# Two transformer blocks: products of the second part and the conditioning of layer 0 issued among the turns of the tiles

## What is computed

```
ada = silu(c) @ W_ada + b_ada
shift_msa, scale_msa, gate_msa, shift_mlp, scale_mlp, gate_mlp = split(ada, 6)
h = layernorm(x) * (1 + scale_msa) + shift_msa
q, k, v = heads(h @ W_qkv + b_qkv)
x = x + gate_msa * (softmax(q * D**-0.5 @ k.T) @ v @ W_proj + b_proj)
```

## Time and profile before

| | us |
|---|---|
| median of three runs | 892.95 |
| lowest, highest | 891.84, 893.7 |
| the profiled execution: its time | 893.41 |
| its span | 891.4 |
| PE busy | 781.1 (88%) |
| DVE busy | 643.1 (72%) |
| ACT busy | 525.9 (59%) |
| POOL busy | 281.8 (32%) |

### The profile page before, as it was taken

One profiled execution on the slowest core, in us unless ns is written; L12 is line 12 of the kernel. 1 busy time (PEld: TensorE's weight loads), 2 busy tenths in 40 slices (PEclk: granted clock), 3 DMA queues, 4 the chain that ended last, 5 costly groups with the idle time before them and its releaser, 6 DMA issues.

```text
span 891.4 us, 16501 instructions
## 1 busy us (share of the span) xinstructions
PE 781.1 (88%) x6096; PEld 363.8 (41%) x6096; DVE 643.1 (72%) x1277; ACT 525.9 (59%) x731; POOL 281.8 (32%) x369
## 2 busy tenths in 40 slices
PE   1569889999988989899898999999979986999996
PEld 0235222222221222222234465566646654566555
DVE  4849888898887898888936955746688897764531
ACT  4433577777776677777785725635547734634640
POOL 4311011325554241102023337241223565342122
PEclk9979799999999999999999999999989996999998
DMA  7302011110111110000040011101676730000000
GB/s 221 83 22 74 21 29 28 28 48 12 41 43 50 45 28 21 21 22 21 2 110 2 11 41 42 22 18 49 155 178 161 175 66 28 8 28 1 26 26 27
DMA packets 52127, 45.35 MB, mean 51 GB/s; under 512 B 23898, under 2 KB 41236, under 8 KB 52055
## 3 DMA queue, kind: packets, MB, share of 16 engines
q1 hardware_dynamic: 47613, 36.35, 15.9%
q10 hardware_dynamic: 4442, 8.04, 2.8%
HBM read 27.66 MB, written 9.46 MB: 42 GB/s over the span
## 4 chain that ended last, share of the span: by engine, by line
PE 55%; DVE 25%; ACT 5%; issue 4%; POOL 4%; DMA 3%; SPq 2%; ACTq 1%; DVEq 0%; POOLq 0%
PE ps L1869 12%; DVE row_max L966 12%; PE ps L1734 10%; PE ps L1695 8%; PE ps L1848 6%; PE ps L1633 4%; PE ps L1686 4%; PE ps L1722 3%; DVE mlp_area L1107 2%; SPq L579 2%; PE ps L1651 2%; PE ps L1602 1%; DVE probs L936 1%; DVE probs L940 1%; ACT mlp_area L1499 1%
## 5 line engine op out<-in xcount | busy, mean ns | idle before, releaser
L966 DVE TENSOR_REDUCE row_max<-ps 128x1 f32<-128x512 f32 x512 | 321.0, 684 | 55.3 <-PE ps L1695 54.2
L1458 ACT ACTIVATE probs<-ps 128x1024 f32<-128x1024 f32 x256 | 249.1, 1018 | 56.9 <-PE ps L1722 56.2
L1695 PE MATMUL ps<-stack_area 54*128 54x512 f16 x512 | 144.6, 390 | 28.3 <-DVE row_max L966 21.2
L1734 PE MATMUL ps<-probs,mlp_area 128*32 128x512 f32 x1024 | 137.2, 608 | 0.0
L1722 PE MATMUL ps<-stack_area 56*128 56x512 f16 x512 | 111.0, 385 | 7.2 <-ACT probs L1458 7.2
L1869 PE MATMUL ps<-w_fc,mlp_area 128*128 128x288 f16 x864 | 109.4, 289 | 4.7 <-DVE mlp_area L1107 4.7
L1695 PEld LDWEIGHTS ps<-stack_area 54*128 54x128 f16 x512 | 35.6, 93 | 187.2 <-DVE row_max L966 173.5
L1848 PE MATMUL ps<-mlp_area,w_fc 128*128 128x512 f16 x504 | 110.8, 379 | 0.8 <-ACT mlp_area L1499 0.8
L1499 ACT ACTIVATE mlp_area<-ps 128x512 f32<-128x512 f32 x72 | 42.9, 595 | 97.9 <-PE ps L1848 95.4
L1869 PEld LDWEIGHTS ps<-w_fc,mlp_area 128*128 128x128 f16 x864 | 84.6, 99 | 28.3 <-DVE mlp_area L1107 3.9
L769 POOL TENSOR_SCALAR neg_scaled<-neg_max 128x16 f32<-128x16 f32 x16 | 4.1, 254 | 271.2 <-DVE neg_max L973 271.2
(11 more groups left out here) (170 smaller groups left out, 1082.1 us busy)
## 6 DMA issues: line engine op xcount, KB each, us to landing
stack_area<-tokens SPq DMA_DIRECT2D x124, 36.0 KB
qkv_rows<-part_area ACTq DMA_DIRECT2D x14, 252.0 KB
qkv_rows<-probs ACTq DMA_DIRECT2D x10, 252.0 KB
x_sb<-in_x SPq DMA_DIRECT2D x4, 576.0 KB, 7.6
w_raw<-in_L_cond_W_fc SPq DMA_DIRECT2D x4, 576.0 KB
tokens<-qkv_rows SPq DMA_DIRECT2D x64, 36.0 KB
v_sb<-qkv_rows SPq DMA_DIRECT2D x16, 144.0 KB
w_raw<-in_L_cond_fc_w SPq DMA_DIRECT2D x4, 576.0 KB
```

What stands on the lines that cost most here:

```text
L966: nc.vector.reduce_max(row_max[:, p % 2, t, j, half:half + 1], bank(bk), AX.X).then_inc(max_done, 1)
L1458: nc.scalar.activation(probs[:, n % 2, 2 * c:2 * c + 2, :].rearrange("p h n -> p (h n)"), ps[:, 2 + 2 * c:4 + 2 * c, :].rearrange("p b n - ...
L1695: nc.tensor.matmul(bank(bk), stacks[rows, p % RING, 0, t * P:(t + 1) * P], stacks[rows, p % RING, 1, half * 512:(half + 1) * 512], start=T ...
L1734: mm = nc.tensor.matmul(bank(6)[at:at + VW, :], v_pad[:, TB * (p // BPAIR) + n, 2 * (p % BPAIR) + j, :], probs[:, n % 2, 2 * c + j, :], st ...
```

## The change

Blocks (1, 0) and (1, 1) leave the slots; PE runs them behind turns 11 and 12, in banks 4 and 5. Block (0, 1) comes behind turn 8 instead of turn 9. PE's round (0, 1) of the conditioning comes behind turn 13, in bank 3, and DVE's two operations for it ahead of the low part of tile 15. ACT takes the blocks in its steps 7, 10, 14 and 15 and issues the six transfers in step 12 instead of 13. The plan of the banks starts from other last users.

```
--- before.py
+++ after.py
@@ -314,9 +314,9 @@
         FIRST_JOB = 1
         WEIGHTS_AT = {-1: (0, 1, 2)}
         STAT_AT = {3: range(8, 12), 4: range(12, 16)}
-        PARTS_AT, TAKES_AT, STORE_AT = (5, 9), (7, 11), 13
+        PARTS_AT, TAKES_AT, STORE_AT = ((0, 5), (0, 8), (1, 11), (1, 12)), (7, 10, 14, 15), 12
         V_AT = {s: (2 * s + 22, 2 * s + 23) for s in range(-11, -3)}
-        ADA_SLOT = -12
+        ADA_AT = 13
         JOBS_AT_FC2 = {0: (0, 2), 3: (0, 2)}
 
         MORE_TILES = {0: (6, 7), 1: (8, 9), 2: (10, 11)}
@@ -422,14 +422,12 @@
         def part_of(s):
             for c in range(QC):
                 p, rest = divmod(s + P_LEADS[c], SLOTS)
-                if rest == 0 and p > 0 and p in FIRST_PAIR:
+                if rest == 0 and p in FIRST_PAIR[2:]:
                     return [("P", FIRST_PAIR.index(p), c)]
             return []
 
         def other_of(s):
             steps = [("V", t) for t in V_AT.get(s, ())]
-            if s == ADA_SLOT:
-                steps.append(("A",))
             if (s + M_LEAD) % SLOTS == 0 and 0 <= s + M_LEAD < NPAIR * SLOTS:
                 steps.append(("M", (s + M_LEAD) // SLOTS))
             if (s - O_LAG) % SLOTS == 0 and s >= O_LAG:
@@ -440,7 +438,7 @@
 
             bank_of, user_before = {}, {}
             last = {0: ("T", NT - 2), 1: ("T", NT - 1), 6: ("P", 0, 0), 7: ("P", 0, 1)}
-            last.update({b: ("T", 0) for b in range(2, 6)})
+            last.update({2: ("T", 0), 3: ("A",), 4: ("P", 1, 0), 5: ("P", 1, 1)})
             at = {b: ALL_SLOTS[0] for b in EARLY_BANKS}
             for s in ALL_SLOTS:
                 maxima, others = maxima_of(s), other_of(s)
@@ -1028,8 +1026,6 @@
                         if step[2:] == (TB - 1, 1, 1):
                             negate_maxima(step[1])
                     for step in other_of(s):
-                        if step[0] == "A":
-                            ada_round(0, 1, BANK_OF[step])
                         if step[0] == "O":
                             normalise_o(step[1], BANK_OF[step])
                     if s >= TAIL_FROM:
@@ -1249,6 +1245,8 @@
                             dve.wait_ge(msa_in[t // TB], 16)
                         if t < NT:
                             normalise(0, t, t % 2, t, t, t // TB, 0)
+                        if t == NT:
+                            ada_round(0, 1, 3)
                         if t:
                             low_part(0, (t - 1) % 2, t - 1)
                     attention()
@@ -1534,7 +1532,8 @@
                         for i in WEIGHTS_AT.get(t, ()):
                             scale_weights(0, i)
                         if t in TAKES_AT:
-                            take_part(0, TAKES_AT.index(t), 6 + TAKES_AT.index(t))
+                            n, c = divmod(TAKES_AT.index(t), QC)
+                            take_part(n, c, 4 + c if n else 6 + c)
                         if t == STORE_AT:
                             act.wait_ge(part_done, 1)
                             for j in range(2):
@@ -1754,8 +1753,6 @@
                     if step[0] == "V":
                         pe.wait_ge(hT_ready[0], step[1] + 1)
                         value_mms(step[1], BANK_OF[step])
-                    if step[0] == "A":
-                        conditioning(0, 1, BANK_OF[step])
                     if step[0] == "M":
                         turn_maxima(step[1], BANK_OF[step])
                     if step[0] == "O":
@@ -1892,12 +1889,15 @@
                 if l == 0:
                     for t in range(NT):
                         turn(0, t % 2, t, t < 2)
-                        if t in PARTS_AT:
-                            c = PARTS_AT.index(t)
-                            pe.wait_ge(w_ready, QKV_JOBS)
-                            pe.wait_ge(ada_sum, 1)
-                            pe.wait_ge(hT_ready[0], TB // 2 * (c + 1))
-                            part_mms(0, c, 6 + c, 0, len(PRODUCTS))
+                        for i, (n, at) in enumerate(PARTS_AT):
+                            if t == at:
+                                c = i % QC
+                                pe.wait_ge(w_ready, QKV_JOBS)
+                                pe.wait_ge(ada_sum, 1)
+                                pe.wait_ge(hT_ready[0], TB // 2 * (c + 1))
+                                part_mms(n, c, 4 + c if n else 6 + c, 0, len(PRODUCTS))
+                        if t == ADA_AT:
+                            conditioning(0, 1, 3)
                     attention()
                 else:
                     head_attention()
```

## The result

Measured: 884.58 us, the median of five runs (883.3 to 887.38), against 892.61 us for the kernel before in the same session (890.79 to 893.7, five runs). The ratio is 0.9916, interval 0.9898 to 0.9934: a gain of 8.0 us (by the interval of the ratio on 892.61, between 5.9 and 9.1). I had forecast 888.4 with a range of 886.1 to 890.8. The first lies wholly beyond my 4.5 us (0.9950); the second holds it, near its edge, and 886.52 us itself lies within my range. So the gain is 5.5 to 8.0 us by the medians of the two sessions, and the size of the miss is known no better than that. The profiled execution took 885.84 us, span 883.8.

The account below looks back on a forecast made before the run. Bound: the turns, then DVE's row of maxima. Turns' end, stretch to the row and row, 59.4 + 9.9 + 16.75 = 86.08, become 61.7 + 1.2 + 18.6 = 81.5; 892.95 - 4.5 = 888.4 us, range 886.1 to 890.8.

Parts of the forecast that it names:

- The bound and the hand-over: From the turns to DVE's gapless row of maxima: starting pair 0's 32 maxima earlier moves everything behind it.
- Step 1: Block (0,1) behind turn 8: starts at 42.2, takes 3.25 us; stack copies issue 2.1 us earlier, at 48.2.
- Step 2: Blocks (1,0) and (1,1) lie beside ACT's issuing and cost nothing; cover 0.2 to 3 us wide before turn 13.
- Step 3: PE's conditioning behind turn 13 joins the turn path: 3.2 us at the low clock, 1.66 at the fast end.
- rival A: Clock high when the conditioning runs: conditioning 1.66 us, gain 6.0 us, 887.0 us; chance 0.28.
- Step 4: Last two turns: DVE's last low part meets POOL's subtraction at the shared port; 0.8 us in full, 0.4 taken.
- Step 5: Start of the maxima: first about 62.1, second about 62.9, then 31 without a gap at 0.60, ending 81.5.
- Step 6: Behind the first maxima: value products (1.89 us) just match DVE, stack transfers arrive in time, bank order costs nothing.
- rival D: Slower: value products at the low clock cost 1.8 us a slot from the third slot on; 899 us; chance 0.04.
- Step 7: Behind the maxima the gain passes on in fixed steps; clock could lose or win up to 1.5 us.
- B: Part of the gain given back behind 86 us by a later clock rise: gain 2 to 3 us, 890.4; chance 0.12.
- C: Nothing comes of it: blocks outlast ACT's issuing or issuing lengthens, turns end 3 us later; about 892; chance 0.06.

Follow-up runs that it names:

- run 1: Changed kernel with the conditioning back in its old slot (-12), blocks, takes and stack copies as changed: 887.49 us against 892.02, ratio 0.9955.
- run 2: Kernel before with only the conditioning moved behind turn 13, blocks and stack copies untouched: 887.66 us against 892.02, ratio 0.9964.
- run 3: The changed kernel once more, unaltered, in a later session for a second profile: 886.52 us against 892.02, ratio 0.9931.
- run 4: Changed kernel with PE's conditioning behind turn 12 and DVE's two operations for it ahead of the low part of tile 13: 887.31 us, ratio 0.995.
- run 7: Changed kernel with 20 added PE products between the maxima of slots -3 to -1, none in the turns: 889.66 us, ratio 0.9974.
- run 8: Changed kernel with PE's conditioning behind turn 12, DVE's two operations where the change put them: 885.49 us, ratio 0.9931.
- run 10: Changed kernel with block (0,1) back behind turn 9 and the stack copies back in step 13: 888.57 us against 893.07, ratio 0.9947.
- the third of before: Third profile of the kernel before, nothing altered: 887.96 us against 893.78, one execution each.
- run 5: Kernel before with added PE products (the table has 50) in PE's idle time between the turns: 888.88 us against 892.06, ratio 0.9958.
- run 6: Changed kernel with 36 added PE products in PE's idle time between the turns: 884.16 us, ratio 0.9908.

## Why the prediction was wrong, by its own steps

- **The bound and the hand-over** were right: the chain enters a row of 31 maxima right behind the turns, and the gain made there passes on unchanged (7.95 us at the negation, 8.05 at the end of pair 0).
- **Step 1, the price of block (0,1), failed.** I priced it at 3.25 us, from the row at 44.34. It took 1.70. The same four products of turn 8, 0.59 us in that profile, took 0.38 in the profiles of all kernels without added products (the change, runs 1 to 4, 7, 8, 10) and in the third of before: the clock is up by then in nine of eleven executions, read by the length of the products. Behind turn 9, after 1.6 to 1.7 us of idle time, it was down again (the third of before, runs 2 and 10); directly behind turn 8 it was still up. So the copies were earlier by 3.4 us, not 2.1. My row came from the same work at another moment, and I took no bound from the other level for it, though I did for the conditioning.
- **Step 2, the cover**, was right: both blocks lie under the issuing. Turn 13 waited for ACT.
- **Step 3, the conditioning, failed**: 1.63 us and not 3.2. This was rival A, to which I gave 0.28. I expected an idle stretch of up to 3.5 us behind the blocks if they ran fast. In the profile of the change they ran 3.10 and 1.72 us, and only 0.95 us of the stretch was left; the clock was up by 52, two microseconds before the conditioning. But in run 3 they ran 1.72 and 1.73 us, the stretch was 2.07 us, and the conditioning took 1.63 us all the same. So the step from an idle stretch of that length to the low level is what failed. The price itself was nearly right (3.10 and 3.09 us at the low level in runs 1 and 2). The thin stretch lay elsewhere: I had PE nearly without gaps from 42.2 on, and it was busy for 1.56 of the 4 us from 44 to 48. The Trainium skill's sentence that "activity releases the throttle" (page "TensorE: Matmul & The Clock Gate", What's actually happening) spoke for this side, and the traces agree: three profiles of this placement (the change, runs 3 and 7) have 1.63 us each. They agree for this place only: later in run 7 PE was busy for 17 us before the clock rose.
- **Step 4, the port**: 0.5 us, taken at 0.4. **Step 5**: second maximum 1.8 us behind the start of the last turn, forecast 2.0; 0.60 a maximum as priced. **Step 6**: no maximum waited for a transfer, and from slot -11 on the value products took 1.89 a pair; in two of three profiles of this placement one pair took 3.3 to 3.5 and cost DVE 1.1 us (rival D for a single slot). **Step 7**: at 0.63 mean clock both before and after, nothing lost or won.
- **The rivals**: A held but was too small, since the same clock also shortened the block; with 1.5 us for that A's 6.0 would have been 7.5. B and C did not occur. D occurred in the small. The range was cut at 886.1 because it was built from A without the block's other level. In the later session the time, 886.52 us, lay in the range, but not by my sum: the block and the conditioning ran at the high level there too.

The order alone is worth about what was forecast (4.7 us, runs 5 and 6). Not shown one by one is how the remaining 1 to 3 us (by session) split between block and conditioning; the first profile says 1.5 and 1.6. Open is also why ACT's six issues take from 4.8 to 6.1 us: I priced them at 6.1 throughout, and in runs 5 and 10 their length moves the end of the stage by 1 us or more.

## What to carry to other kernels

A price read off one profile for PE's work holds for the clock that this work had at that moment. When a step is moved, price it at both levels, and look at what PE does just ahead of its new place. Filling a producer's wait (here ACT's six issues) with another engine's work pays twice if it also brings the clock up for what comes next; work added for the clock's sake alone went with a gain of 3.2 us in the turns of the kernel before, with none that the medians show in those of the changed kernel (run 6), and lost 4 to 5 us in run 7, where the clock fell in spite of it. And a wait with a fixed place in the order need not have a fixed length: read it in more than one profile.

## What was not expected of the hardware

The column of the granted clock reads 1.00 in all profiles until the first recorded fall, also where the products have the length of the low level (block (0,0), 3.25 us at 36 in the changed kernel, where seven products at the high level take 1.70 to 1.72). The length of a known product tells the level, the column does not. And a PE without a gap in its busy time is no guarantee of a rise: in run 7 it stayed at 0.50 for 17 us.
